# A product moved from GpSimd to VectorE in a planned schedule, with the order planned anew

## The chip, the cores and the metric

One core of a Trainium2 chip (trn2) runs the kernel. Its engines are TensorE (PE, which shows in the profile as PE for matmuls and PEld for weight loads), VectorE (DVE), ScalarE (ACT), GpSimd (POOL) and SyncE (SP, which here only issues DMAs). The metric is the device time of one execution in microseconds; a kernel is run several times and the median is given.

## The reference

A layer of 2048 tokens with 512 channels: half a feed-forward network (FFN1), a selective state-space scan, half a second feed-forward network (FFN2), each behind a layer norm and with a residual.

```python
x = x + 0.5 * ffn(layernorm(x), w1, w2, w3)
x = x + ssm(layernorm(x), W_x, W_dt, b_dt, A_log, D_param)
x = x + 0.5 * ffn(layernorm(x), w1, w2, w3)

# ffn: weights rounded to -1, 0, 1
hidden = sigmoid(x @ q(w1).T) * (x @ q(w2).T);  out = hidden @ q(w3).T

# ssm, x here is the normed x ("xln" in the kernel)
xz = x @ W_x.T                      # 128 columns dt_raw, 16 columns b, 16 columns c
dt = softplus(dt_raw @ W_dt.T + b_dt)
h[t] = exp(dt[t] * a) * h[t-1] + dt[t] * b[t] * x[t]     # a state for each of 16 n and 512 channels
y[t] = sum over n of h[t] * c[t];   out = y + x * D_param
```

The change concerns `dt * x`, called u, which is the same for all 16 states n and is multiplied by b for each.

## The kernel before

Channels lie on the partitions: 512 channels are 4 groups of 128, so a tile of one chunk is 128 x 4 x 256 = 128x1024. The tokens go in 8 chunks of 256. The body is a loop over chunks c and, in each, over 16 scan steps s, one for each state. A step is spread over engines:

- ACT computes the decays exp(dt * a) of the next step into PSUM in two halves (L767) and, between them, adds the carry from the chunk before to the first column of the scan's input (L787).
- POOL multiplies u by row b of a step two ahead (`times_b`, L1201, into the ring `dbx`; called a multiplication below) and issues the DMA that adds a product to the sum over n (`add_prod`, L1214). `add_y` (L1219) adds the sum of the odd products to that of the even ones.
- DVE runs the scan in two halves (L988, scan s.0 and s.1), multiplies the states by row c (`times_c`, L1001, product s) and saves the last column (L1006).
- SP loads the rows of b and c and stores the outputs.

Beside the scan of chunk c run, a piece at a time, FFN2 of chunk c-1, FFN1 of chunk c+1 and three layer norms: LN2 (ahead of FFN2, of chunk c-1), LN1 (ahead of the scan of chunk c+1) and LN0 (ahead of FFN1 of chunk c+3). A layer norm is a round over the engines: mean (PE), centre (DVE, L933), square (ACT, L687), fold of the squares (POOL, L308 and L310; LN0 has a fold of x as well), var (PE), std (ACT, L705), recip (DVE, L937), spread (PE), norm (DVE, L941), and for the two FFNs the split into two f16 parts, x_hi (ACT, L713) and x_lo (POOL, L1175). Mean, variance and spread of all three go through one PSUM bank, `stat`. Behind LN1 come xz (PE: dt_raw, b and c), the reads of dt_raw and of b and c (ACT, L734 and L740), z0 and z1 (PE) and the softplus into dt (ACT, `z_read`, L753, four pieces), again by way of `stat`.

An FFN is 11 up tiles of 16 matmuls (up1[h] of FFN1, up2[h] of FFN2), gated by ACT's tanh (L720) and DVE's product (hid1, hid2, L953), split by ACT (hid_hi, L728) and POOL (hid_lo, L1181; lo1, lo2 in the tables), then four down products of 22 matmuls (down1, down2) and DVE's residual in two pairs (res1, res2, L960).

Each engine runs its list in order, and waits on semaphores. Where a piece stands in the list of its engine is written in four tables, AT_PE, AT_ACT, AT_DVE and AT_POOL: an entry 10*s + p is place p (0 to 3) of scan step s, with tables of their own for the first and the last chunk. On PE, which has no part in the scan, the tables give the order alone. The program walks the places and, at each, calls the pieces that are due, in a fixed order.

The product u of chunk c+1 is computed on POOL at its place `u` by `dt_times_xln` (L1189), one instruction over 128x1024; `u` has two buffers. The first multiplication of a chunk waits for `u_done`. In chunk 0, DVE computes u in two halves ahead of the loop (`first_u_of`, L1047).

Of the kernel before, what the change touches and what calls it, by code (L numbers as in the profile page):

```python
# [17 lines left out]
ALU = mybir.AluOpType  # L18
# [4 lines left out]
NS, RANK = 16, 128  # L23
# [22 lines left out]
    down1=[123, 130, 131, 133], down1_first=[142, 143, 152, 152], down2=[153, 153, 153, 153],  # L46
    down2_last=[153, 153, 153, 153], mean0=152, mean0_first=153, mean1=140, mean1_first=153, mean2=123,
    mean2_last=153, spread0=153, spread0_first=153, spread1=143, spread1_first=153, spread2=132,
    spread2_last=153, up1=[40, 40, 53, 53, 53, 83, 83, 83, 101, 111, 112],
    up1_first=[20, 23, 23, 23, 53, 73, 73, 92, 133, 140, 142],  # L50
    up2=[140, 140, 142, 143, 150, 151, 152, 152, 152, 152, 153],
    up2_last=[153, 153, 153, 153, 153, 153, 153, 153, 153, 153, 153], var0=153, var0_first=153, var1=142,
    var1_first=153, var2=131, var2_last=153, xz=150, xz_first=153, z0=151, z0_first=153, z1=152, z1_first=153)
AT_ACT = dict(
    bc_read=102, bc_read_first=111, d_xln=152, d_xln_first=152, dt_raw=102, dt_raw_first=112,
    gate1=[1, 10, 12, 12, 21, 30, 30, 40, 40, 41, 42], gate1_first=[0, 0, 0, 10, 12, 20, 22, 22, 40, 42, 42],
    gate2=[81, 92, 110, 110, 120, 121, 130, 140, 140, 141, 142],
    gate2_last=[61, 70, 82, 90, 91, 101, 102, 111, 112, 120, 122],
    hi1=[10, 12, 21, 30, 31, 31, 40, 41, 41, 50, 50], hi1_first=[2, 11, 11, 31, 32, 40, 41, 50, 50, 50, 51],
    hi2=[112, 112, 112, 112, 130, 131, 131, 141, 141, 142, 142],  # L60
    hi2_last=[71, 81, 100, 101, 111, 112, 112, 121, 130, 130, 130], square0=130, square0_first=130, square1=81,
    square1_first=90, square2=60, square2_last=30, std0=141, std0_first=140, std1=90, std1_first=92, std2=61,
    std2_last=32, x_hi0=151, x_hi0_first=150, x_hi2=71, x_hi2_last=50, z_read=[112, 112, 120, 120],
    z_read_first=[121, 121, 121, 121])
AT_DVE = dict(
    centre0=130, centre0_first=131, centre1=81, centre1_first=82, centre2=52, centre2_last=23,
    hid1=[3, 12, 20, 22, 30, 32, 40, 41, 42, 43, 51], hid1_first=[1, 2, 10, 12, 22, 30, 40, 41, 42, 50, 51],
    hid2=[90, 110, 112, 120, 130, 131, 132, 141, 142, 143, 150],
    hid2_last=[63, 82, 92, 100, 102, 110, 112, 120, 122, 123, 123], norm0=151, norm0_first=150, norm1=93,
    norm1_first=102, norm2=71, norm2_last=50, recip0=142, recip0_first=142, recip1=92, recip1_first=101,  # L70
    recip2=70, recip2_last=42, res1=[63, 72], res1_first=[63, 80], res2=[153, 153], res2_last=[102, 133])
AT_POOL = dict(
    add_y=31, add_y_last=11, fold_sq0=141, fold_sq0_first=140, fold_sq1=82, fold_sq1_first=82, fold_sq2=51,
    fold_sq2_last=32, fold_x0=92, fold_x0_first=110, lo1=[11, 30, 40, 42, 42, 42, 42, 42, 42, 42, 50],
    lo1_first=[21, 22, 31, 32, 41, 41, 41, 41, 41, 41, 41],
    lo2=[131, 131, 141, 141, 150, 150, 150, 150, 150, 150, 150],
    lo2_last=[91, 102, 110, 120, 121, 131, 131, 131, 131, 131, 131], u=132, u_first=132, x_lo0=152,
    x_lo0_first=152, x_lo2=80, x_lo2_last=51)


# [13 lines left out]
def macaron(nc, xT, w_xT, w_dtT, b_dt, a_log, d_param, w1T, w2T, w3T, outT):  # L94
    ctx = ExitStack()
    with ctx:
# [833 lines left out]
        def _(dve):  # L930
# [162 lines left out]
            def beside_scan(c, par, now):  # L1093
# [15 lines left out]
                if not last(c):  # L1109
# [4 lines left out]
                    if now == at(AT_DVE, c, "norm1"):  # L1114
                        normalise(1, c + 1, xln)
# [219 lines left out]
```

## Time and profile before

| | |
|---|---|
| median of 3 runs | 792.58 us (787.21 to 796.45) |
| the profiled execution | 794.82 us, of which the span of the trace is 793.0 us |
| mean granted TensorE clock | 0.914 |
| busy, share of the span | PE 80%, PEld 66%, DVE 81%, ACT 72%, POOL 81% |
| u on POOL (L1189) | 7 instructions, 22.4 us in all, mean 3206 ns |
| multiplications on POOL (L1201) | 127, mean 2720 ns |
| scans on DVE (L988) with a carry | 224, mean 1277 ns |

The span runs from the first to the last instruction of the core, and the execution's time is a little longer. Busy times of POOL are rough: an instruction that stands behind a DMA issue is recorded from its own issue on, so neighbours overlap. In the trace, the scan of chunk 0 begins near 80 us, that of chunk 7 ends near 749 us; before it lie the quantisation of the weights and FFN1 of chunk 0, behind it the last LN2 and FFN2. A chunk in the middle takes about 88 us.

### The profile page before, as it was taken

Reading aid. Unit: us, or ns where it says so; the run is one execution under the profiler, and the core shown is the slowest. Engines: PE = TensorE matmul, PEld = TensorE weight load, DVE = VectorE, ACT = ScalarE, POOL = GpSimd, SP = SyncE. Lnnn points to the kernel's source line nnn. Section 1 sums busy time; section 2 is a strip of 40 time slices with the busy share of each in tenths; the row PEclk is TensorE's granted clock in tenths of the full one; section 3 lists DMA queues with packets and bytes.
Section 4 is the critical chain, followed back from the end, with each engine's and each line's share of the span. In section 5 each row is a group of like instructions: output and inputs, shape, how many; then the busy total and the mean of one; then the engine's idle time right before and its main releaser. Section 6 shows DMA issues by size and latency. Waiting matters only on the chain.

```text
span 793.0 us, 14028 instructions
## 1 busy us (share of the span) xinstructions
PE 636.6 (80%) x4872; PEld 523.8 (66%) x4872; DVE 640.2 (81%) x825; ACT 569.3 (72%) x1344; POOL 644.4 (81%) x523
## 2 busy tenths in 40 slices
PE   4798775397889987997889987988889888348898
PEld 4577653286668765876667765876667766236787
DVE  3863898899877998699878997798959997599831
ACT  5864756878786879587886879678877779377441
POOL 0181999999988999699988999799988989689812
PEclk8699997599989999899999999999989999659999
DMA  9501678887748878497748777588829766968100
GB/s 355 167 1 44 155 173 177 213 185 180 160 103 186 167 169 188 89 215 180 166 98 196 162 161 186 138 172 183 199 57 211 160 139 161 208 154 167 28 27 27
DMA packets 42438, 121.06 MB, mean 153 GB/s; under 512 B 5888, under 2 KB 14848, under 8 KB 42368
## 3 DMA queue, kind: packets, MB, share of 16 engines
q0 software_dynamic: 18864, 68.69, 46.5%
q1 hardware_dynamic: 23504, 51.49, 19.5%
q8 instruction: 38, 0.62, 0.3%
q14 instruction: 32, 0.26, 0.1%
HBM read 47.03 MB, written 4.46 MB: 65 GB/s over the span
## 4 chain that ended last, share of the span: by engine, by line
PE 30%; ACT 19%; POOL 16%; DVE 16%; issue 15%; DMA 3%; DVEq 1%; ACTq 0%; POOLq 0%
PE work L413 22%; DVE states L988 9%; POOL shared L1201 8%; PE stat L413 6%; ACT decay L767 6%; POOL shared L1214 3%; DVE shared L1001 3%; ACT shared L787 2%; ACT tanh L720 2%; DMA shared<-shared 2%; POOL square L308 2%; ACT hid_hi L728 2%; POOL hid_lo L1181 1%; ACT dt L753 1%; DVE hid L953 1%
## 5 line engine op out<-in xcount | busy, mean ns | idle before, releaser
L413 PE MATMUL work<-x_hi,q 128*128 128x256 f16 x1408 | 333.8, 284 | 39.3 <-DVE hid L953 21.3
L1201 POOL TENSOR_TENSOR shared<-u,b_row 128x1024 f32<-128x1024 f32 x127 | 345.2, 2720 | 0.5
L413 PE MATMUL work<-x_lo,q 128*128 128x256 f16 x1408 | 333.1, 284 | 0.0
L767 ACT ACTIVATE decay<-dt,a_neg 128x256 f32<-128x256 f32 (+1 forms) x512 | 220.7, 464 | 102.1 <-DVE states L988 101.4
L988 DVE TENSOR_TENSOR_SCAN states<-decay,last_state,shared 128x512 f32<-128x512 f32 x224 | 279.8, 1277 | 9.3 <-ACT shared L787 3.5
L1181 POOL TENSOR_TENSOR hid_lo<-hid,hid_hi 128x256 f16<-128x256 f32 x176 | 147.8, 1082 | 96.2 <-ACT hid_hi L728 96.0
L413 PEld LDWEIGHTS work<-x_hi,q 128*128 128x128 f16 x1408 | 143.7, 102 | 75.8 <-DVE hid L953 33.9
L413 PE MATMUL work<-hid_hi,q 128*128 128x256 f16 x693 | 159.2, 279 | 8.3 <-POOL hid_lo L1181 6.1
L1001 DVE TENSOR_TENSOR shared<-states,c_row 128x1024 f32<-128x1024 f32 x128 | 155.7, 1217 | 7.8
L413 PE MATMUL work<-hid_lo,q 128*128 128x256 f16 x693 | 158.7, 278 | 0.0
L413 PEld LDWEIGHTS work<-x_lo,q 128*128 128x128 f16 x1408 | 143.3, 102 | 22.0
L1214 POOL DMA_DIRECT2D shared<-shared x124 | 140.1, 1130 | 8.7 <-DMA shared<-shared 3.3
L953 DVE SCALAR_TENSOR_TENSOR hid<-tanh,work 128x256 f32<-128x256 f32 x176 | 71.9, 410 | 37.1 <-ACT tanh L720 36.8
L720 ACT ACTIVATE tanh<-work 128x256 f32<-128x256 f32 x176 | 63.2, 370 | 37.7 <-PE work L413 33.6
L413 PEld LDWEIGHTS work<-hid_hi,q 128*128 128x128 f16 x693 | 70.1, 101 | 20.5 <-DVE hid L953 6.0
L413 PEld LDWEIGHTS work<-hid_lo,q 128*128 128x128 f16 x693 | 69.3, 100 | 10.0
L728 ACT ACTIVATE hid_hi<-hid 128x256 f16<-128x256 f32 x176 | 66.9, 408 | 9.2 <-DVE hid L953 8.9
L787 ACT ACTIVATE shared<-last_state,shared,first_decay 128x1 f32<-128x1 f32 x224 | 73.0, 373 | 0.0
L413 PE MATMUL stat<-mean_w,square 128*128 128x1 f32 x96 | 16.6, 281 | 39.5 <-POOL square L310 35.8
L413 PE MATMUL stat<-shared,mean_w 128*128 128x256 f32 x120 | 31.1, 404 | 19.3 <-DMA shared<-shared 12.1
L413 PEld LDWEIGHTS stat<-mean_w,square 128*128 128x128 f32 x96 | 14.8, 225 | 46.5 <-POOL square L310 42.1
L988 DVE TENSOR_TENSOR_SCAN states<-decay,shared 128x512 f32<-128x512 f32 x32 | 38.1, 1220 | 4.0 <-POOL shared L1298 2.0
(118 smaller groups left out, 665.1 us busy)
## 6 DMA issues: line engine op xcount, KB each, us to landing
shared<-shared POOLq DMA_DIRECT2D x131, 512.0 KB, 5.3
b_row<-bc_dram SPq DMA_DIRECT2D x32, 512.0 KB, 5.8
c_row<-bc_dram SPq DMA_DIRECT2D x32, 512.0 KB, 6.2
x_in<-xT SPq DMA_DIRECT2D x8, 512.0 KB, 7.0
outT<-shared SPq DMA_DIRECT2D x7, 512.0 KB, 5.5
shared<-w1T SPq DMA_DIRECT2D x4, 704.0 KB, 8.5
shared<-w2T SPq DMA_DIRECT2D x4, 704.0 KB, 12.1
shared<-w3T SPq DMA_DIRECT2D x3, 768.0 KB, 13.4
```

The costliest lines, as they stand in the source:

```text
L308: engine.tensor_tensor(dst[:, 0:2, :], src[:, 0:2, :], src[:, 2:4, :], ALU.add).then_inc(summed, 1)
L413: return nc.tensor.matmul(out, lhsT, rhs, start=start, stop=stop)
L720: nc.scalar.activation(tanh[:, h % 3, :], bank_of(which, h)[:, 0, :], ACT.Tanh, scale=0.5 / X_SCALE).then_inc(tanh_done, 1)
L728: nc.scalar.activation(hid_hi[:, h, :], hid[:, hid_slot(which, h), :], ACT.Copy).then_inc(hi_done, 1)
L767: ins = nc.scalar.activation(decay[pair][:, j, j:TC], dt[:, par, k, j:TC], ACT.Exp, scale=a_neg[:, k, n:n + 1])
L787: nc.scalar.activation(column, last_state[:, n, k:k + 1], ACT.Identity, scale=first_decay[:, par, j, n:n + 1], bias=column).then_inc(carry ...
L953: nc.vector.scalar_tensor_tensor(out=hid[:, hid_slot(which, h), :], in0=tanh[:, h % 3, :], scalar=1.0, in1=bank_of(which, h)[:, 1, :], op0 ...
L988: nc.vector.tensor_tensor_scan(out=states[:, two, :].rearrange("p k t -> p (k t)"), data0=decay[pair][:, :, :].rearrange("p k t -> p (k t) ...
L1001: nc.vector.tensor_tensor(prod_of(c, n), states[:, :, :], bcast(c_row[:, group % 2, n % ROWS, :]), ALU.mult).then_inc(prod_done, 1)
L1181: nc.gpsimd.tensor_tensor(hid_lo[:, h, :], hid[:, hid_slot(which, h), :], hid_hi[:, h, :], ALU.subtract).then_inc(lo_done, 1)
L1201: nc.gpsimd.tensor_tensor(dbx[:, g % DBX_RING, :, :], u[:, par, :, :], bcast(b_row[:, group % 2, n % ROWS, :]), ALU.mult).then_inc(dbx_don ...
L1214: nc.gpsimd.dma_start(total, prod_of(c, n), accum_op=ALU.add).then_inc(added(c, n)[0], 16)
```

## The change

The product u of the chunk that comes next is taken off POOL's list and put on DVE's, at a place of its own: behind product 12 (entry 123), in chunk 0 behind scan 14.0 (entry 141). On DVE it waits for all four pieces of the softplus, and for the multiplications of the chunk before the last, which read the same buffer. All four tables are new. In a middle chunk the order of PE becomes ..., mean1, up2[0] to up2[2], var1, up2[3], spread1, xz, z0, up2[4], up2[5], z1, mean0, up2[6] to up2[8], var0, spread0, up2[9], up2[10], down2. It was ..., mean1, up2[0], up2[1], var1, up2[2], spread1, up2[3], xz, up2[4], z0, up2[5], z1, mean0, up2[6] to up2[9], var0, spread0, up2[10], down2.

```diff
 AT_PE = dict(
-    down1=[123, 130, 131, 133], down1_first=[142, 143, 152, 152], down2=[153, 153, 153, 153],
-    down2_last=[153, 153, 153, 153], mean0=152, mean0_first=153, mean1=140, mean1_first=153, mean2=123,
...
-    up2=[140, 140, 142, 143, 150, 151, 152, 152, 152, 152, 153],
...
+    down1=[133, 133, 140, 141], down1_first=[142, 150, 150, 151], down2=[153, 153, 153, 153],
+    down2_last=[153, 153, 153, 153], mean0=152, mean0_first=153, mean1=143, mean1_first=153, mean2=133,
...
+    up2=[143, 143, 143, 150, 151, 151, 152, 152, 152, 153, 153],
...
 AT_ACT = dict(
...
-    hi2_last=[71, 81, 100, 101, 111, 112, 112, 121, 130, 130, 130], square0=130, square0_first=130, square1=81,
-    square1_first=90, square2=60, square2_last=30, std0=141, std0_first=140, std1=90, std1_first=92, std2=61,
...
+    hi2_last=[82, 92, 92, 110, 110, 111, 111, 112, 120, 121, 122], square0=122, square0_first=131, square1=72,
+    square1_first=82, square2=51, square2_last=30, std0=132, std0_first=141, std1=90, std1_first=100, std2=60,
...
 AT_DVE = dict(
-    centre0=130, centre0_first=131, centre1=81, centre1_first=82, centre2=52, centre2_last=23,
...
-    hid2_last=[63, 82, 92, 100, 102, 110, 112, 120, 122, 123, 123], norm0=151, norm0_first=150, norm1=93,
-    norm1_first=102, norm2=71, norm2_last=50, recip0=142, recip0_first=142, recip1=92, recip1_first=101,
-    recip2=70, recip2_last=42, res1=[63, 72], res1_first=[63, 80], res2=[153, 153], res2_last=[102, 133])
+    centre0=130, centre0_first=133, centre1=80, centre1_first=90, centre2=51, centre2_last=22,
...
+    hid2_last=[80, 83, 92, 93, 102, 103, 112, 113, 120, 122, 130], norm0=150, norm0_first=150, norm1=93,
+    norm1_first=103, norm2=70, norm2_last=60, recip0=141, recip0_first=150, recip1=92, recip1_first=102,
+    recip2=63, recip2_last=50, res1=[63, 71], res1_first=[80, 81], res2=[153, 153], res2_last=[113, 113], u=123,
+    u_first=141)
 AT_POOL = dict(
...
-    lo2=[131, 131, 141, 141, 150, 150, 150, 150, 150, 150, 150],
-    lo2_last=[91, 102, 110, 120, 121, 131, 131, 131, 131, 131, 131], u=132, u_first=132, x_lo0=152,
-    x_lo0_first=152, x_lo2=80, x_lo2_last=51)
...
+    lo2=[131, 141, 141, 141, 141, 142, 151, 151, 151, 151, 151],
+    lo2_last=[100, 111, 111, 121, 121, 122, 122, 130, 131, 131, 131], x_lo0=152, x_lo0_first=152, x_lo2=72,
+    x_lo2_last=71)
...
+            def dt_times_xln(c, par):
+
+                dve.wait_ge(z_read, KD * (c + 1))
+                if c > 1:
+                    dve.wait_ge(dbx_done, NS * (c - 1))
+                nc.vector.tensor_tensor(u[:, par, :, :], dt[:, par, :, :], xln[:, :, :], ALU.mult).then_inc(u_done, 1)
+
...
+                    if now == at(AT_DVE, c, "u"):
+                        dt_times_xln(c + 1, 1 - par)
...
-            def dt_times_xln(c, par):
-                pool.wait_ge(z_read, KD * (c + 1))
-                nc.gpsimd.tensor_tensor(u[:, par, :, :], dt[:, par, :, :], xln[:, :, :], ALU.mult).then_inc(u_done, 1)
-
...
-                    if now == at(AT_POOL, c, "u"):
-                        dt_times_xln(c + 1, 1 - par)
```

## Rows read from the trace of the kernel before

**Rows 1.** Busy us, 228 to 317: length, PE, PEld, DVE, ACT, POOL; clock, DMA

```profile
228.00:317.00 89.00, 77.04 (x596) 63.56 (x597) 75.98 (x102) 69.55 (x169) 81.09 (x68) 0.94 0.74 162
```

**Rows 2.** DVE's waits, 228 to 317 us: waiter, releaser, us, times, longest

```profile
DVE shared L960 <- PE work L413: 3.9, 1, 3.9
DVE hid L953 <- ACT tanh L720: 3.3, 1, 3.3
DVE rstd L937 <- ACT std L705: 3.1, 2, 1.6
DVE xln L941 <- PE stat L413: 1.2, 1, 1.2
DVE centred L933 <- PE stat L413: 1.0, 1, 1.0
DVE states L988 <- ACT shared L787: 0.6, 1, 0.6
```

**Rows 3.** Timeline of PE, 286 to 318 us: start, length, operation, wait before

```profile
287.07 0.61 PE L413 MATMUL stat<-mean_w,square 128*128 128x1 f32 x4 [1.55 <-POOL square L310]
...
304.57 0.70 PE L413 MATMUL stat<-square,mean_w 128*128 128x256 f32 x2 [0.93 <-ACT dt L753]
...
313.19 0.61 PE L413 MATMUL stat<-mean_w,square 128*128 128x1 f32 x4 [0.45 <-POOL square L310]
316.62 1.22 PE L413 MATMUL stat<-ident,rstd 128*128 128x128 f32 x4 [2.83 <-DVE rstd L937]
```

**Rows 4.** Timeline of POOL, 300 to 312 us

```profile
301.24 2.94 POOL L1201 TENSOR_TENSOR shared<-u,b_row 128x1024 f32<-128x1024 f32 x1
...
305.40 3.25 POOL L1189 TENSOR_TENSOR u<-dt,xln 128x1024 f32<-128x1024 f32 x1
308.73 2.37 POOL L1201 TENSOR_TENSOR shared<-u,b_row 128x1024 f32<-128x1024 f32 x1
311.05 1.27 POOL L308 TENSOR_TENSOR square<-square 128x512 f32<-128x512 f32 x1
```

**Rows 5.** Timeline of ACT, 303 to 316 us

```profile
303.67 0.84 ACT L753 ACTIVATE dt<-stat,bdt 128x256 f32<-128x256 f32 x2
...
308.52 1.05 ACT L687 ACTIVATE square<-centred 128x1024 f32<-128x1024 f32 x1
...
314.81 1.28 ACT L705 ACT_TABLE_LOAD   x1
```

**Rows 6.** Groups of DVE by line: count, busy us, mean ns

```profile
L941 DVE TENSOR_TENSOR xln<-centred,stat 128x1024 f32<-128x1024 f32 x7 | 8.5, 1219 | 6.9 <-PE stat L413 6.9
...
L1047 DVE TENSOR_TENSOR u<-dt,xln 128x512 f32<-128x512 f32 x2 | 1.4, 686 | 2.3 <-ACT dt L852 2.3
```

**Rows 7.** Timelines of POOL and of DVE, 34 to 55 us

```profile
34.47 0.67 POOL L1181 TENSOR_TENSOR hid_lo<-hid,hid_hi 128x256 f16<-128x256 f32 x1 [33.00 <-ACT hid_hi L728]
...
45.35 9.07 POOL L1181 TENSOR_TENSOR hid_lo<-hid,hid_hi 128x256 f16<-128x256 f32 x7
...
45.89 1.81 DVE L1041 SCALAR_TENSOR_TENSOR q<-shared,thr,q 128x1536 f16<-128x1536 f32 x1
```

**Rows 8.** Busy time by engine in three stretches of 2 us

```profile
294.00:296.00 2.00, 2.00 (x10) 1.15 (x9) 1.87 (x4) 1.60 (x5) 2.00 (x3) 1.00 0.11 20
318.00:320.00 2.00, 2.00 (x12) 1.38 (x10) 0.52 (x3) 1.43 (x5) 1.29 (x2) 0.50 0.18 33
326.00:328.00 2.00, 2.00 (x21) 1.79 (x19) 1.72 (x3) 2.00 (x6) 2.00 (x2) 1.00 0.51 98
```

**Rows 9.** Timeline of PE in chunk 0: xz

```profile
127.58 3.78 PE L413 MATMUL stat<-xln,wx 128*128 128x256 f32 x8 [1.31 <-DVE xln L941]
```

**Rows 10.** DVE's waits, 78 to 142, 580 to 658 and 678 to 752 us

```profile
DVE centred L933 <- PE stat L413: 2.0, 1, 2.0
...
DVE hid L953 <- ACT tanh L720: 5.1, 2, 3.3
...
DVE centred L933 <- PE stat L413: 3.4, 1, 3.4
```

## What I expect, and why

> **What bounds the kernel now.** The granted clock and the page come first: one core, all four compute engines busy for 72 to 81% of the span (table above), no single one full. So I cut the span into chunks of tokens. Between 228 and 317 us, one steady chunk, DVE works 76 of 89 us and POOL 81 [rows 1]. POOL's share says less than it seems: its instructions overlap in the record with the DMA issues behind them. The next view is the list of DVE's waits in that chunk [rows 2]. DVE runs its list in order, the same list in every chunk; so the length of a chunk is DVE's work plus those waits, and it is there that a change must show. They are: 3.9 us for the residual's last pair (res2[1], behind PE's down products), 3.3 for the last gated tile (hid2[10]), 1.6 twice for the reciprocal of LN0's deviation (the stretch holds two chunk ends), 1.2 for LN1's spread, 1.0 for LN0's mean, 0.6 for the carry. The timeline of PE shows the chain behind most of them: the three layer norms of a chunk take turns in one PSUM bank (stat), each a round through PE, DVE, ACT, POOL and PE again. At the chunk's end PE waits 0.45 us for POOL's fold of the squares (var0) and 2.83 for the reciprocal (spread0) [rows 3]. It then still has one up tile and all of down2 to do, for which DVE waits in turn.
>
> **The product u.** POOL's seven u products go. One is issued at 305.40 and the next multiplication starts at 308.73, the fold of LN0's squares at 311.05 [rows 4]; ACT had those squares at 308.52 + 1.05 = 309.57 [rows 5]. So on POOL u holds var0 back by 1.5 us, no more. DVE adds seven u. The half-size form, the same operation on the same tensors, took 686 ns in chunk 0, and a full 128x1024 product with one operand in PSUM 1219 [rows 6]: 1.22 to 1.37 us, I take 1.22. Its place is after product 12 and ahead of centre0. It needs the last softplus, which ended at 303.67 + 0.84 = 304.51 [rows 5], and LN0's mean, for which DVE waited 1.0 us there, was waiting for the same softplus [rows 3]. So u runs in that wait and in the 0.6 us for the carry behind it. 1.6 us of waits become 1.22 of work: -0.3 a chunk (-0.4 if both go wholly, +1.2 if neither does). Queued behind u's new wait on DVE are centre0, hid2[4] and scan 13, which all waited for that softplus or for ACT behind it already. The second new wait, for an older chunk's multiplications, is long met. On POOL the next chunk's first multiplication now waits for DVE's u, and the fold is queued behind it. By the softplus u ends near 305.8, the multiplication (2.37) at 308.2, before the squares are there; POOL waits, but nobody for it.
>
> u reads two operands in SBUF, which no other DVE instruction of the scan does. The quantisation at the start does, and there the rows show a price: seven hid_lo tiles took 9.07 us where a lone one took 0.67, that is 4.4 too many, while three such DVE operations ran, the first of them 1.81 long [rows 7]. Such an operation and a reading POOL exclude each other. In the steady chunk POOL's multiplication 15, 301.24 + 2.94, has ended before u may start, and what follows is one hid_lo, a DMA issue and the multiplication that waits for u. I charge nothing here, and keep 0 to 2.4 us (one multiplication) a u for the range.
>
> The Trainium skill ("SBUF — State Buffer", Who interferes with whom) says that a DVE instruction with two SBUF inputs contends with a GpSimd instruction that reads SBUF, and that whichever issued first keeps the shared port to its end. By that rule u could stand behind a whole multiplication in each chunk, which is the second rival below; by the order in the rows it stands behind nothing. The trace agrees that there is a lock.
>
> **The new order.** Read against the old one (a table entry 10s+p is the place p of scan step s), four moves matter.
>
> LN1: centre1 goes ahead of scan 8.0, square1 ahead of ACT's step 8, var1 behind a third up2 tile. Before, PE stood 1.55 us at var1 [rows 3]; the third tile now fills that. Spread1 is then ready as DVE comes to norm1, whose wait of 1.2 us shrinks. Bounds 0 and -1.2, I take -0.9, since the fold on POOL still lies between. xz then follows spread1 without the tile that stood there, so PE waits about as long as norm1 takes, 1.2 us, twice over with the read of dt_raw. That delays up2 tiles, not the chain.
>
> LN0's deviation: std0 goes in ACT from behind the next step's decays and carry to ahead of them. Before, ACT reached it at 314.81 with the variance ready since 313.8 [rows 3, 5]; with the 1.5 us from POOL it can run near 312.5. recip0 goes one scan forward in DVE. Its wait of 1.6 us should fall to 0.3: -1.3 (bounds 0 and -1.6).
>
> The chunk's end: up2[9] goes behind spread0, where only up2[10] and down2 stood. A tile of 16 matmuls costs 1.5 us at full clock (21 in 2 us) and 2.7 at half (12 in 2 us) [rows 8]; the restart after spread0 runs at half clock (0.50, 1.2 GHz) in both orders, for the same stretch, so I charge PE 1.8. DVE has one scan and one gated tile (about 1.7 us) more between recip0 and res2[1] than before, but at the half clock both tiles come late: I take +0.5. Bounds: +1.8 if nothing covers the tile, -2.5 if the shorter stand of PE before spread0 keeps the clock up.
>
> A steady chunk so gives -0.3 - 0.9 - 1.3 + 0.5 = -2.0, and five of them (chunks 1 to 5) -10. Chunk 0 has waits of 2.0 us at centre0 [rows 10]; centre0 goes later and u in: -0.5 (-1.8 to +1.2). Chunk 6 has no LN0; its hid waits are 5.1 us [rows 10], of which 3.3 belong to the end of the chunk before, and the rest, 1.8, is where u goes; norm1 stands there as in the others: -0.6 - 0.9 = -1.5. In chunk 7 centre2 waits 3.4 us for the last sums of products [rows 10]; POOL's last multiplication of chunk 6 now stands ahead of five hid_lo tiles, so the DMA that adds the last product leaves up to 2.4 us earlier, and centre2 goes ahead of one product (1.2): -1. What moves in the last chunk's FFN2 ends where it did: hid2[10] stays behind product 12. Sum: -10 - 0.5 - 1.5 - 1 = -13 us. Start and tail are untouched. On the profiled execution, 793.0 of span in 794.82, that is 781.8; it lies 2.2 over the median of the three runs, 792.58, from which I forecast 780.
>
> **The rivals.** First, the waits only change their place. After spread0 PE has the same down2 and one tile more, and res2[1] ends the chunk; if spread0 doesn't come earlier by as much as the three waits shrink, +1.8 in place of +0.5 and -0.6 in place of -1.3 leave 0.0 a chunk, and -3 in all: 790 us. For it: res2[1] is the largest wait of the chunk, and PE's. Against it: spread0 itself hung on the reciprocal.
>
> Second, the lock. If POOL runs ahead in the new order so that a multiplication is under way at each u, DVE stands 1.2 us on the mean and POOL 1.2: about 1.5 of each pair reaches the chain, 7 x 1.5 = 10: 790 us. Against it: POOL can't start the next chunk before u.
>
> Third, slower: the clock falls ahead of xz. PE now stands before xz and again before z0, where up tiles filled it. In chunk 0, after a stand of 1.31 us, eight xz matmuls took 3.78 [rows 9], 16 would take 7.6; in the steady chunk, at clock 1.00, ten of them fit in 2 us [rows 8], so 16 take half of that or less. At the lower of the two levels (1.2 GHz) the chain through softplus, u and centre0 is then 3.8 us longer in six chunks: 792.6 - 13 + 23 = 802. It decides as soon as xz runs at 0.50. Against it: up2[0] to up2[3] run on without a stand just ahead.
>
> **How the numbers follow.** Forecast 0.50, moved waits 0.23, lock 0.10, clock 0.17. 1% is 7.9 us, about what a measurement here can tell, as the three runs lie 9 us apart. Most of the forecast's case lies under 784.7, a little of it over; the first two rivals are no change; the third is slower: 0.47, 0.35, 0.18. The range takes in the clock's case to 802. Below, if half of the bound for PE's clock came true, 5 x 2.5 more, it ends at 768.
>
> **What would show it.** In the trace after: u on DVE at 1.2 to 1.3 us, right behind the last softplus; no wait at the carry of scan 13; POOL's fold of LN0 less than 0.3 us behind its squares; DVE's waits at recip0 and norm1 under 0.5; res2[1] at 3 to 5. Wrong would be u longer than 1.5 us, xz at clock 0.50, or a sum of res2[1] and hid2[10] waits over 9 us a chunk.

## The result and the profile after

The changed kernel takes 801.34 us, the median of ten runs (798.11 to 803.56), against 794.40 us for ten runs of the kernel before on the same chip (787.21 to 796.45): a ratio of 1.0100, with a 95% interval of 1.0068 to 1.0133. It is slower by 1%, where I had forecast 780 us. Its profiled execution took 798.11 us with a span of 796.3. That is the shortest of its ten, 3.2 us under their median, so the trace below shows 3.3 us of a loss that the medians put at 6.9; where the other executions lose the rest was not recorded (their mean granted clock was 0.914 to 0.925, that of the profiled one 0.936).

The page's first part says almost nothing: POOL's share falls from 81% to 79%, DVE's rises from 81% to 82%.

```profile
PE 633.6 (80%) x4872; PEld 520.8 (65%) x4872; DVE 651.4 (82%) x832; ACT 570.6 (72%) x1344; POOL 628.9 (79%) x516
```

What says where the time went is one instruction followed through both traces. DVE's product s of chunk c (the multiplication of the states with C) occurs 128 times at the same place of the algorithm, so the differences of its start times cut both spans into comparable sections. "Chunk 0" is from its first product to the first of chunk 1, "chunks 1 to 5" from there to the first of chunk 6, "6 and 7" to the last product of all. The start lies before, the tail behind. The sections of all kernels of this study, from one profiled execution each, in us:

| kernel | start | chunk 0 | chunks 1 to 5 | chunks 6 and 7 | tail | span |
|---|---|---|---|---|---|---|
| before | 84.27 | 72.12 | 441.54 | 149.88 | 45.19 | 793.0 |
| after | 84.03 | 77.65 | 436.81 | 152.89 | 44.92 | 796.3 |
| e1 u alone, old order | 83.44 | 72.73 | 440.28 | 150.78 | 44.87 | 792.1 |
| e2 new order, u on POOL | 82.62 | 77.25 | 438.04 | 150.91 | 47.18 | 796.0 |
| e3 chunk 0 as before | 85.48 | 74.78 | 438.16 | 153.09 | 45.09 | 796.6 |
| e4 tiles ahead of xz | 83.62 | 78.32 | 433.14 | 151.77 | 47.05 | 793.9 |
| e5 first gate later | 82.60 | 75.57 | 440.99 | 152.97 | 47.07 | 799.2 |
| e6 chunk 7 as before | 85.39 | 78.12 | 438.27 | 150.36 | 45.06 | 797.2 |
| e7 both ends as before, tiles | 84.21 | 73.54 | 433.07 | 149.25 | 45.03 | 785.1 |
| e8 the same, u on POOL | 83.63 | 72.74 | 436.38 | 149.99 | 45.06 | 787.8 |
| e9 e7 with chunk 0 as changed | 83.21 | 75.25 | 435.83 | 149.27 | 45.04 | 788.6 |
| e10 e7 with half an u more | 83.67 | 75.29 | 431.23 | 149.95 | 45.26 | 785.4 |
| e11 e7 with up2[9] earlier | 84.20 | 73.62 | 430.46 | 149.39 | 44.93 | 782.6 |
| e12 up2[4] ahead of xz | 83.50 | 77.99 | 473.05 | 158.79 | 47.47 | 840.8 |
| e13 up2[3] ahead of xz | 84.70 | 77.74 | 432.26 | 151.32 | 45.08 | 791.1 |

No kernel changes the start or the tail: their spread (82.6 to 85.5; 45 or 47) is what one execution does by itself, and kernels that are alike in the middle differ there by up to 2.8 (e7, e9). So a smaller difference of one section is not read as an effect by itself, only where the rows below or the times say the same.

The middle gains 4.73 us, less than half of the 10 that I forecast. Chunk 0 loses 5.53 and chunks 6 and 7 lose 3.01.

**The middle.** DVE's waits in a steady chunk (first view, 231 to 320 us: waiter, releaser, us, times, longest) answer to [rows 2]; the second view is the busy time of that stretch, as in [rows 1].

```profile
DVE shared L961 <- PE work L414: 4.5, 2, 4.1
DVE hid L954 <- ACT tanh L721: 2.0, 3, 1.3
DVE u L1050 <- ACT dt L754: 0.9, 1, 0.9
DVE rstd L938 <- ACT std L706: 0.7, 1, 0.7
DVE centred L942 <- PE stat L414: 0.6, 1, 0.6
```
```profile
231.00:320.00 89.00, 77.00 (x603) 63.03 (x602) 78.08 (x101) 70.01 (x170) 79.05 (x68) 0.96 0.73 161
```

The wait for LN0's deviation fell from 1.6 to 0.7, that of norm1 from 1.2 to 0.6, hid2[10]'s from 3.3 to 1.7 in this chunk; res2's rose from 3.9 to 4.5; u has a wait of its own. Over chunks 1 to 5, DVE's idle time fell from 12.76 to 10.17 us a chunk (worked out from all of DVE's rows there), and its busy time rose from 75.55 to 77.19: 0.95 a chunk are left.

The timeline of TensorE (PE) shows where u's wait comes from. Here are the eight xz matmuls of all six chunks, and one chunk's rounds ahead of them (start, length, operation, wait before); [rows 3] and [rows 8] answer to them.

```profile
207.54 3.50 PE L414 MATMUL stat<-xln,wx 128*128 128x256 f32 x8 [1.78 <-DVE xln L942]
...
289.93 0.58 PE L414 MATMUL stat<-mean_w,square 128*128 128x1 f32 x4
...
293.11 0.71 PE L414 MATMUL stat<-ident,rstd 128*128 128x128 f32 x4 [0.51 <-DVE rstd L938]
295.61 3.47 PE L414 MATMUL stat<-xln,wx 128*128 128x256 f32 x8 [1.78 <-DVE xln L942]
299.01 2.08 PE L414 MATMUL stat<-xln,wbc 128*32 128x256 f32 x8
...
383.82 2.94 PE L414 MATMUL stat<-xln,wx 128*128 128x256 f32 x8 [1.78 <-DVE xln L942]
...
470.68 1.99 PE L414 MATMUL stat<-xln,wx 128*128 128x256 f32 x8 [1.78 <-DVE xln L942]
...
557.59 1.99 PE L414 MATMUL stat<-xln,wx 128*128 128x256 f32 x8 [1.78 <-DVE xln L942]
...
644.33 3.56 PE L414 MATMUL stat<-xln,wx 128*128 128x256 f32 x8 [1.78 <-DVE xln L942]
```
```profile
294.00:296.00 2.00, 0.39 (x2) 0.37 (x3) 2.00 (x4) 1.38 (x5) 2.00 (x3) 0.99 1.05 201
296.00:298.00 2.00, 2.00 (x6) 1.57 (x5) 1.93 (x2) 1.21 (x4) 1.92 (x3) 0.50 0.71 135
```

In every chunk TensorE now stands 1.78 us ahead of xz. In four of six the matmuls then run at a granted clock of 0.50 (1.2 GHz) and take 2.9 to 3.6 us; in two they take 1.99. The eight behind them (wbc) are at full speed again. DVE's rows at u show what that costs: 0.89 us of waiting in just those four chunks, none in the two others (the second row).

```profile
308.77 1.22 DVE L1050 TENSOR_TENSOR u<-dt,xln 128x1024 f32<-128x1024 f32 x1 [0.89 <-ACT dt L754]
...
482.69 1.40 DVE L1050 TENSOR_TENSOR u<-dt,xln 128x1024 f32<-128x1024 f32 x1
```

So u does not wait for the stand alone; it waits for the clock behind it. The traces of one order bear this out without moving a tile. In the changed kernel and in e3, e5 and e6 below, which leave these tiles where they are, xz ran at the lower clock for most of its length in 17 of the 24 chunks 1 to 6 (2.9 to 3.7 us) and at full speed in 7 (1.99). From product 12 to product 13 DVE takes 7.9 to 8.0 us in each of the 17 and 6.9 in each of the 7: a chunk at the lower clock pays 1.06 us there, 0.89 at u and 0.17 at the carry behind it. What decides which chunks it hits is not shown.

**The end of chunk 0**, on DVE, TensorE and POOL:

```profile
143.27 1.22 DVE L934 TENSOR_TENSOR centred<-x_in,stat 128x1024 f32<-128x1024 f32 x1 [2.53 <-PE stat L414]
...
145.54 1.21 DVE L1050 TENSOR_TENSOR u<-dt,xln 128x1024 f32<-128x1024 f32 x1
...
150.07 0.17 DVE L938 RECIPROCAL rstd<-std 128x2 f32<-128x2 f32 x1 [0.76 <-ACT std L706]
151.55 1.22 DVE L942 TENSOR_TENSOR centred<-centred,stat 128x1024 f32<-128x1024 f32 x1 [1.31 <-PE stat L414]
...
161.35 0.42 DVE L954 SCALAR_TENSOR_TENSOR hid<-tanh,work 128x256 f32<-128x256 f32 x1 [2.22 <-ACT tanh L721]
```
```profile
139.04 2.04 PE L414 MATMUL stat<-dt_raw,wdt 128*128 128x256 f32 x4 [2.67 <-ACT dt L754]
142.01 1.22 PE L414 MATMUL stat<-square,mean_w 128*128 128x256 f32 x2 [0.93 <-ACT dt L754]
148.72 1.02 PE L414 MATMUL stat<-mean_w,square 128*128 128x1 f32 x4 [5.49 <-POOL square L311]
```
```profile
145.67 2.19 POOL L309 TENSOR_TENSOR square<-square 128x512 f32<-128x512 f32 x1 [3.94 <-ACT square L688]
```

The chain mean0, squares, fold, var0, recip0, norm0 lies on DVE's path here. It starts late (mean0 at 142.01, where it was at 139.94 before), its fold takes 2.19 us beside u, where it takes 1.27 alone, and DVE waits for it three times (2.53 us at centre0, 0.76 at recip0, 1.31 at norm0). Of the 5.53 us that chunk 0 loses, 3.9 are waits of DVE and 1.6 its work, u above all. The last row of DVE is hid1[0] of chunk 1, which the new table sets ahead of the first product (place 2 for 3): the product stands behind its wait of 2.22 us.

**Chunk 7** keeps its wait at centre2 (3.4 in [rows 10], now one product earlier). The last product of chunk 6, for whose sum centre2 waits, and centre2, before and after:

```profile
671.25 1.22 DVE L1001 TENSOR_TENSOR shared<-states,c_row 128x1024 f32<-128x1024 f32 x1
...
693.84 1.22 DVE L933 TENSOR_TENSOR centred<-shared,stat 128x1024 f32<-128x1024 f32 x1 [3.37 <-PE stat L413]
```
```profile
672.47 1.23 DVE L1002 TENSOR_TENSOR shared<-states,c_row 128x1024 f32<-128x1024 f32 x1
...
694.92 1.22 DVE L934 TENSOR_TENSOR centred<-shared,stat 128x1024 f32<-128x1024 f32 x1 [3.70 <-PE stat L414]
...
719.41 0.42 DVE L954 SCALAR_TENSOR_TENSOR hid<-tanh,work 128x256 f32<-128x256 f32 x1 [1.18 <-ACT tanh L721]
```

From the one to the other it takes 22.6 us before and 22.5 after. The third row is a wait of FFN2's gates that chunk 7 did not have.

### The profile page after: what moved, and what is told of

Same layout as the page of the kernel before. It is cut to its first block, busy times and chain, and to the rows that moved or that the text cites. A ratio compares the mean times of both kernels' runs of the same rounds, so it can differ in the third digit from the quotient of the medians.

```text
span 796.3 us, 14034 instructions
## 1 busy us (share of the span) xinstructions
PE 633.6 (80%) x4872; PEld 520.8 (65%) x4872; DVE 651.4 (82%) x832; ACT 570.6 (72%) x1344; POOL 628.9 (79%) x516
## 4 chain that ended last, share of the span: by engine, by line
PE 30%; DVE 21%; POOL 17%; ACT 15%; issue 13%; DMA 3%; DVEq 1%; ACTq 0%; POOLq 0%
PE work L414 21%; DVE states L989 11%; PE stat L414 8%; POOL hid_lo L1191 7%; POOL shared L1207 5%; ACT decay L768 5%; DVE shared L1002 4%; DMA shared<-shared 2%; ACT shared L788 2%; ACT tanh L721 2%; POOL shared L1220 1%; ACT hid_hi L729 1%; POOL square L309 1%; ACT dt L754 1%; POOL shared L1253 1%
## 5 line engine op out<-in xcount | busy, mean ns | idle before, releaser
L414 PE MATMUL work<-x_hi,q 128*128 128x256 f16 x1408 | 324.3, 280 | 36.6 <-DVE hid L954 17.6
L414 PE MATMUL work<-x_lo,q 128*128 128x256 f16 x1408 | 323.6, 279 | 0.0
L1191 POOL TENSOR_TENSOR hid_lo<-hid,hid_hi 128x256 f16<-128x256 f32 x176 | 153.7, 1214 | 66.0 <-ACT hid_hi L729 66.0
L414 PEld LDWEIGHTS work<-x_hi,q 128*128 128x128 f16 x1408 | 141.2, 100 | 66.3 <-DVE hid L954 25.2
L414 PE MATMUL work<-hid_hi,q 128*128 128x256 f16 x693 | 155.4, 274 | 22.1 <-POOL hid_lo L1191 18.6
L414 PE MATMUL work<-hid_lo,q 128*128 128x256 f16 x693 | 155.4, 274 | 0.0
L414 PEld LDWEIGHTS work<-x_lo,q 128*128 128x128 f16 x1408 | 141.1, 100 | 20.2
L309 POOL TENSOR_TENSOR square<-square 128x512 f32<-128x512 f32 x21 | 33.7, 1603 | 12.8 <-ACT square L688 12.7
L1185 POOL TENSOR_TENSOR x_lo<-centred,x_hi 128x1024 f16<-128x1024 f32 x14 | 34.6, 2473 | 6.0 <-ACT x_hi L714 6.0
```

Source lines behind the costliest of these rows:

```text
L309: engine.tensor_tensor(dst[:, 0:2, :], src[:, 0:2, :], src[:, 2:4, :], ALU.add).then_inc(summed, 1)
L414: return nc.tensor.matmul(out, lhsT, rhs, start=start, stop=stop)
L1191: nc.gpsimd.tensor_tensor(hid_lo[:, h, :], hid[:, hid_slot(which, h), :], hid_hi[:, h, :], ALU.subtract).then_inc(lo_done, 1)
```

## Experiments

My theory after the result: the order costs at both ends and through the clock at xz, and the move of u is not the matter. The ratios below stand against the kernel before on the same chip, five rounds each. The runs were made on several chips, on which the kernel before took 792.5 to 795.3 us, so between runs of different chips the ratios compare better than the medians.

**e1: u alone, in the old order.**

```diff
 AT_DVE = dict(
...
+    u=130, u_first=131)
 AT_POOL = dict(
...
-    u=132, u_first=132,
```

> The old order in every list, with u alone moved from POOL to DVE, right ahead of centre0 (place 130, in chunk 0 place 131). If u is what made the change slow, because its 1.22 us on DVE is not covered, seven of them put it 4 to 9 us over the kernel before (798 to 803). If u is covered by DVE's waits for LN0's mean and the carry, as in my prediction, and the new order is what cost the time, it comes out 2 to 8 us under the kernel before, for LN0's fold on POOL is no longer behind u: 786 to 792, with POOL's fold in the middle chunks right behind ACT's squares.

795.49 us, ratio 1.0031 (1.0010 to 1.0051): between my two ranges, so neither came. All sections lie within 1.3 us of before: by itself the move gains nothing. The group of u on DVE (duration min/median/max in ns, first and last start) shows one reason:

```profile
L1048 DVE TENSOR_TENSOR u<-dt,xln x7: 1226/2020/3074, 139.5 to 654.7; 128x1024 f32<-128x1024 f32 x7
```

At this place POOL is still reading in most chunks, and u takes 2.02 us (the median) where it takes 1.21 alone. That is my second rival's lock, real in an order that was not the changed one's.

**e2: the new order with u on POOL.** The changed tables, with u and u_first taken from DVE's table and put at 132 in POOL's.

> The new order in every list, with u back on POOL at its old place (132, behind the DMA issue of product 12). If the new order lost the time, it is as slow as the changed kernel or slower by up to 8 us (800 to 809): the 5 us lost at the end of chunk 0 and the first xz matmuls at half clock stay. If u on DVE lost it, it falls back to the kernel before or under it (787 to 796).

798.31 us, 1.0063 (1.0040 to 1.0086): between the two ranges, nearer to the order's. Chunk 0 loses 5.1 us, as in the changed kernel (5.5), and xz runs at the lower clock in four of six chunks here too: those losses belong to the order. The profiled spans of e2 and of the changed kernel are equal (796.0, 796.3), the timed ratios 0.4% apart: the changed kernel's trace is of its shortest execution, 0.4% under its median, and that of e2 lies at its median (797.79).

**e3: chunk 0 in its old places** (all that end in _first), u_first at 131.

```diff
-    up1_first=[11, 23, 33, 33, 43, 112, 113, 121, 140, 140, 140],
+    up1_first=[20, 23, 23, 23, 53, 73, 73, 92, 133, 140, 142],
...
-    centre0=130, centre0_first=133,
+    centre0=130, centre0_first=131,
...
-    u_first=141)
+    u_first=131)
```

> The changed kernel with the lists of chunk 0 as they were before, and u of that chunk on DVE right ahead of centre0 (131). In the traces the changed kernel falls 5.3 us behind between product 13 of chunk 0 and product 0 of chunk 1. If the lists of chunk 0 do that, this run is 4 to 6 us faster than the changed kernel (795 to 797), and its product 0 of chunk 1 comes within 1.5 us of that of the kernel before (156.4). If u in chunk 0 does it by itself, the time stays at 799 to 803.

796.48 us, 1.0041 (1.0021 to 1.0062), as the theory said. Products 12 to 15 of chunk 0 take 16.91 us (19.62 changed, 16.27 before). Behind them, though, the step to chunk 1 still takes 6.23, against 4.10 before: hid1[0] has no place of its own for chunk 0.

**e4: TensorE's tiles around LN1 as before.**

```diff
-    down1=[133, 133, 140, 141],
+    down1=[113, 113, 120, 121],
...
-    up2=[143, 143, 143, 150, 151, 151, 152, 152, 152, 153, 153],
+    up2=[122, 122, 123, 130, 131, 132, 133, 133, 133, 153, 153],
...
-    var1=150, xz=151, z0=151, z1=152, spread1=151,
+    var1=123, xz=131, z0=132, z1=133, spread1=130,
```

> The changed kernel with PE's list around LN1 as before: up2[2] between var1 and spread1, up2[3] between spread1 and xz, up2[4] between xz and z0, up2[5] ahead of z1. In the changed kernel eight xz matmuls of a middle chunk took 3.47 us, against 1.89 before. If the stand of PE ahead of xz is what halves the clock there, the eight take 1.9 again and six chunks gain about 1.5 us each: 790 to 794. If the tile ahead of xz costs the chain as much as the clock does (one tile is 1.7 us), the time stays within 3 us of the changed kernel (798 to 804), with the clock up.

794.36 us, 1.0009 (0.9988 to 1.0029), at the edge of the theory's range. xz takes 1.9 to 2.0 us in all six chunks without a wait, u waits nowhere, and chunks 1 to 5 are 3.7 us shorter than in the changed kernel. The clock's theory holds, but three tiles moved at once (up2[2] to up2[4]), so e12 and e13 were made.

**e12 and e13: one step of that alone.** In the changed kernel's order "var1, up2[3], spread1, xz, z0, up2[4]", e12 puts up2[4] ahead of xz; e13 instead puts up2[2] behind var1 and up2[3] behind spread1.

```diff
 e12
-    up2=[143, 143, 143, 150, 151, 151, 152, 152, 152, 153, 153],
+    up2=[142, 142, 142, 143, 150, 151, 152, 152, 152, 153, 153],
 e13
-    up2=[143, 143, 143, 150, 151, 151, 152, 152, 152, 153, 153],
+    up2=[142, 142, 143, 150, 151, 151, 152, 152, 152, 153, 153],
 both
-    mean1=143, var1=150, spread1=151,
+    mean1=142, var1=143, spread1=150,
```

> The changed kernel with one tile moved: in each of chunks 1 to 6 TensorE issues up2[4] between spread1 and xz instead of behind z0; nothing else is moved against anything. Theory that what the new order loses in the middle is TensorE idle for 1.8 us ahead of xz and then on the lower clock: xz takes 1.9 us without a wait in all chunks (3.5 us in four of six before), u waits no more (0.9 us in four chunks), and the run is 2 to 4 us shorter than the changed kernel (797 to 799). Rival, that the gain of the kernel with the tiles ahead of the projections came from its other moved tiles (those ahead of LN2's sums): within 1 us of the changed kernel (800.5 to 802). Second rival, that the tile makes xz itself late, since it takes 1.9 us and the idle time is 1.8 us: xz ends where it did with the lower clock, and u waits 0.5 us or more still.

842.27 us, 1.0619 (1.0581 to 1.0656): neither theory. TensorE's timeline shows the moved tile behind spread1:

```profile
299.43 0.71 PE L414 MATMUL stat<-ident,rstd 128*128 128x128 f32 x4 [0.51 <-DVE rstd L938]
306.06 0.40 PE L414 MATMUL work<-x_hi,q 128*128 128x256 f16 x1 [5.92 <-DVE hid L954]
```

The tile needs an accumulator that a gate multiply (hid) frees, and that stands on DVE behind norm1 and a product. TensorE's list is in order, so xz and the later tiles wait behind it, and DVE then stands 5.5 to 7.1 us at a later gate, in each of six chunks. The run told nothing of the clock.

> The changed kernel with two tiles of chunks 1 to 6 each put one place later on TensorE: up2[2] behind var1 instead of ahead of it, up2[3] behind spread1 and so ahead of xz; unlike up2[4] of the run before, whose accumulator waits for a gate multiply that stands behind norm1 on VectorE, these have their accumulators free in time. Theory that the idle 1.8 us ahead of xz and the lower clock behind it are what the new order loses in the middle: xz takes 1.9 to 2.0 us in all chunks, waits under 0.2 us, u does not wait for dt, and the run is 2 to 4 us shorter than the changed kernel (797 to 799). Rival, that the gain of the kernel with the tiles ahead of the projections came from its other moved tiles: within 1 us of the changed kernel (800.5 to 802).

792.77 us, 1.0002 (0.9976 to 1.0029). These tiles have their accumulators:

```profile
288.15 0.61 PE L414 MATMUL stat<-mean_w,square 128*128 128x1 f32 x4 [1.55 <-POOL square L311]
...
291.38 1.22 PE L414 MATMUL stat<-ident,rstd 128*128 128x128 f32 x4 [0.45 <-DVE rstd L938]
...
294.63 1.89 PE L414 MATMUL stat<-xln,wx 128*128 128x256 f32 x8
```

xz takes 1.9 to 2.0 us in all chunks from 1 on, u's wait is gone, and TensorE stands 1.55 us at var1 instead, as before the change [rows 3]. The ratio falls by 1.0%, chunks 1 to 5 by 4.55 us, and they now gain 1.86 a chunk on the kernel before. So it was these two tiles; the rival that other tiles of e4 did it falls. The time fell by 8 us, more than the 2 to 4 that I expected; the two traces are 5.2 apart, and 3.2 more is what the changed kernel's trace lies under its median.

**e5: hid1[0] behind the first product again.**

```diff
-    hid1=[2, 12, 20, 21, 30, 31, 32, 40, 50, 50, 50],
+    hid1=[3, 12, 20, 21, 30, 31, 32, 40, 50, 50, 50],
```

> The changed kernel with one number put back: the first gate multiply of a chunk's first feed-forward (hid1[0]) stands behind the product of step 0 again (place 3 for 2). Theory that the end of chunk 0 lost time in two places, of which one is this multiply, which stands ahead of chunk 1's first product and waits 2.22 us there for its tanh: in chunk 1 the product of step 0 comes about 2.1 us sooner, later chunks show no wait at either place, so the run is 1 to 2 us shorter than the changed kernel (about 799.5 to 800.5). Rival, that the wait only passes on: the same wait shows up behind that product in chunk 1 and the run is within 0.5 us of the changed kernel.

797.50 us, 1.0047 (1.0030 to 1.0064), 0.5% below the changed kernel and lower than expected. The step from product 15 to the next chunk takes 4.10 us again for 6.52. But 1.5 us of waits return behind the product (0.80 at hid1[0], 0.75 at a carry), and the profiled execution, the longest of its seven, shows no gain by the chunk's end. That the place costs is shown, its size is not.

**e6: chunk 7 in its old places.**

```diff
-    centre2=51, centre2_last=22,
+    centre2=51, centre2_last=23,
...
-    hid2_last=[80, 83, 92, 93, 102, 103, 112, 113, 120, 122, 130],
+    hid2_last=[63, 82, 92, 100, 102, 110, 112, 120, 122, 123, 123],
```

> The changed kernel with the places of the last chunk (all that end in _last) as before. Theory that the new places of chunk 7 lose 1.5 us between its first and its last product (68.08 against 66.62 us): the run is 1 to 2.5 us shorter than the changed kernel (799 to 800.5), and chunk 7 takes 66.5 to 67. Rival, that chunk 7 is long for what chunk 6 hands it and not for its own order: chunk 7 stays at 68 and the run within 0.5 us of the changed kernel.

797.26 us, 1.0036 (1.0022 to 1.0051), lower than expected. From its first product to its last, chunk 7 takes 65.47 us (68.08 changed, 66.62 before). Its wait at centre2 is shorter than in both, but centre2 stands no earlier behind chunk 6's last product (22.3 us):

```profile
675.85 1.23 DVE L1001 TENSOR_TENSOR shared<-states,c_row 128x1024 f32<-128x1024 f32 x1
...
698.18 1.22 DVE L933 TENSOR_TENSOR centred<-shared,stat 128x1024 f32<-128x1024 f32 x1 [2.23 <-PE stat L413]
```

The wait is shorter because chunk 7's first product comes 0.9 us later behind that product than before, 10.8 us for 9.9. From centre2 to chunk 7's last product it takes 53.97 us, as before, where the changed kernel takes 56.47: that 2.5 is the new last table's.

**e7 and e8: both ends as before, tiles ahead of xz; then u back on POOL.**

```diff
 e7: tables ..._first and ..._last as before, up2, down1, xz as in e4, and
+    u_first=132, hid1=[3, 12, 20, 21, 30, 31, 32, 40, 50, 50, 50],
 e8: e7, and
-    u=123, u_first=132)
 AT_POOL = dict(
+    u=132, u_first=132,
```

> The changed kernel's middle chunks alone: the places of chunk 0 and of chunk 7 as before (the product dt by xln right behind centre0 in chunk 0), hid1[0] behind the product of step 0, and TensorE's first up tiles again ahead of and between the projections. Theory that the loss sits at both ends and at the projections' clock, and that the middle is worth 1.7 us for each of five chunks: 786 to 789, 5 to 8 us under the kernel before, with u at 1.2 to 1.4 us and no wait for dt in chunks 1 to 6. Rival, that what is mended at one place is waited for at the next (chunk 0's end, the tail's feed-forward): 792 to 795, no better than the kernel with the tiles alone (794.4).

786.78 us, 0.9907 (0.9890 to 0.9925): faster than both kernels, as the theory said. The medians differ by 7.9 us from before, and so do the spans.

> The run before with one thing changed: the product dt by xln goes back to GpSimd (place 132). Theory that the move itself is worth little in either order, since what VectorE gains in waits it pays in its own 1.2 us: within 2 us of the run before (786 to 791), with waits at centre0 of about 1 us and at the carry of scan 13 of 0.55 us in each chunk. Rival, that the move carries the gain of the middle chunks: 4 to 8 us slower than the run before.

792.16 us, 0.9962 (0.9943 to 0.9980). The move of u is worth 5.4 us here by the medians and 4.4 by the ratios (2.7 between the two traces): my theory falls and the rival holds. With u on POOL, centre0 and the carry wait again (0.5 and 0.56 us in chunks 2 to 4). By e1 the move alone gains nothing in the old order; it gains in this one.

**e9: e7 with chunk 0 as changed.** All places that end in _first as in the change.

> The best run so far (786.8 us: both ends as before, tiles ahead of the projections) with chunk 0 in the changed kernel's order again (all places that end in _first). Theory that the new order of chunk 0's last three steps, with the product dt by xln behind centre0 and the first scan of step 14, and recip0 and norm0 later, costs by itself: from the product of step 12 of chunk 0 to the first of chunk 1 it takes about 24 us for 22, and the run is 1.5 to 3 us slower (788.5 to 790). Rival, that only the first gate multiply cost there, which stays behind its product here: within 0.7 us of 786.8.

790.88 us, 0.9945 (0.9926 to 0.9963): over e7 by 4 us by the medians and 3 by the ratios, a little more than the theory's. Products 12 to 15 of chunk 0 take 19.64 us for 17.85. With e3, the first table's cost stands apart from hid1[0]'s.

**e10: half an u more on DVE.**

```diff
+                nc.vector.tensor_tensor(u_again[:, :, :], dt[:, par, 0:2, :], xln[:, 0:2, :], ALU.mult)
                 nc.vector.tensor_tensor(u[:, par, :, :], dt[:, par, :, :], xln[:, :, :], ALU.mult).then_inc(u_done, 1)
```

> The best run so far (786.8 us) with one more multiply ahead of each product dt by xln on VectorE: the same operands, half as long, into a buffer that nobody reads (it adds work and changes no result). It measures what VectorE's time is worth at that place: by the row of a 512-element operation it takes about 0.7 us, seven times. Theory that u sits on the path there since nothing waits at scan 13 any more: 4 to 5 us slower (791 to 792). Rival, that u and its neighbours lie in waits, as my forecast had it for the old order: within 1.5 us (786 to 788.5).

788.66 us, 0.9917 (0.9903 to 0.9930). The seven multiplies take 6.9 us (median 0.87), of which 1.9 (by the medians) or 0.8 (by the ratios) reach the time. My theory here, that u lies wholly on the path, falls, and the rival holds by the ratios. The rows of recip0 in chunk 2, of e7 and of e10, show where it went in a steady chunk: the next wait of DVE shrinks.

```profile
313.52 0.17 DVE L936 RECIPROCAL rstd<-std 128x2 f32<-128x2 f32 x1 [0.72 <-ACT std L704]
```
```profile
312.83 0.17 DVE L937 RECIPROCAL rstd<-std 128x2 f32<-128x2 f32 x1 [0.26 <-ACT std L705]
```

The shortest steady chunks last 85.6 us in both (u behind the multiply takes 1.21 us there, and 1.4 without it). Chunk 0, where u is followed by no such wait, pays instead: 75.29 us for 73.54, as the multiply takes 0.67 and u behind it 2.28 for 1.21, beside POOL's fold.

```profile
143.92 2.28 DVE L1050 TENSOR_TENSOR u<-dt,xln 128x1024 f32<-128x1024 f32 x1
```

**e11: e7 with up2[9] ahead of var0 and spread0 again.**

```diff
-    up2=[122, 122, 123, 130, 131, 132, 133, 133, 133, 153, 153],
+    up2=[122, 122, 123, 130, 131, 132, 133, 133, 133, 152, 153],
```

> The best run so far (786.8 us) with the last up tile but one of the second feed-forward (up2[9]) issued ahead of var0 and spread0 instead of behind both, as the kernel before had it. My forecast charged its new place 0.5 us a chunk. By that theory this run is about 2.5 us faster (784 to 785) and the wait of 0.5 to 1.8 us at hid2 before the last product is gone. Rival: a tile of 32 matmuls takes 3.5 us where TensorE waits 0.5 us for the folded squares, so var0 comes 3 us late, norm0 and x_hi with it, and the run is 2 to 10 us slower.

784.54 us, 0.9872 (0.9857 to 0.9887), the fastest of all. TensorE's rounds of LN0 in chunk 2, e7 first, then e11:

```profile
310.86 0.61 PE L412 MATMUL stat<-mean_w,square 128*128 128x1 f32 x4 [0.49 <-POOL square L309]
313.74 0.71 PE L412 MATMUL stat<-ident,rstd 128*128 128x128 f32 x4 [2.27 <-DVE rstd L936]
```
```profile
311.88 0.50 PE L412 MATMUL stat<-mean_w,square 128*128 128x1 f32 x4
312.94 0.71 PE L412 MATMUL stat<-ident,rstd 128*128 128x128 f32 x4 [0.55 <-DVE rstd L936]
```

The tile fills the stand at spread0 (2.27 to 0.55), recip0 waits 0.2 us longer, and the wait at hid2 ahead of the last product is 0.5 in every chunk, where it went up to 1.8. A gain of 2.6 us in five chunks (2.8 by the ratios of e7 and e11), as large as my term said.

The cause, though, is the clock. In the 4 us behind spread0 the granted clock of e7 is 1.00 in chunks 2 and 3 and 0.57 to 0.78 in chunks 1, 4 and 5; that last gate waits 0.52 us in the two and 1.5 to 1.8 in the three (e7, chunks 2 and 4):

```profile
318.81 0.42 DVE L952 SCALAR_TENSOR_TENSOR hid<-tanh,work 128x256 f32<-128x256 f32 x1 [0.52 <-ACT tanh L719]
...
491.56 0.42 DVE L952 SCALAR_TENSOR_TENSOR hid<-tanh,work 128x256 f32<-128x256 f32 x1 [1.83 <-ACT tanh L719]
```

In e11, with the stand at 0.55 us, the clock there is 1.00 in all five. Its chunks all last 85.8 to 86.0 us, counted from product 10 to product 10; in e7 the two at 1.00 last 85.6 and the other three 86.6 to 87.2.

## Why the forecast was wrong

Term by term, in us of the profiled execution (by the medians the loss is 6.9 us and not 3.3); the last column is what the term gives once its cause is taken away:

| term | forecast | measured | in which run it is mended |
|---|---|---|---|
| chunks 1 to 5 | -10 | -4.7 | -9.3 (e13), -11.1 (e11) |
| chunk 0 | -0.5 | +5.5 | +1.4 (e7) |
| chunks 6 and 7 | -2.5 | +3.0 | +0.5 (e6), -0.6 (e7) |
| start, tail | 0 | -0.5 | |
| sum | -13 | +3.3 | -7.9 (e7), -10.4 (e11) |

**The step that failed in the middle** is the sentence "That delays up2 tiles, not the chain." I saw that xz would lose the tile ahead of it and costed TensorE's stand, by itself rightly at nothing, but not the clock behind it; I had that as the third rival, and "xz at clock 0.50" as a sign of being wrong. Its mechanism came true, in four of six chunks, at another price: not 3.8 us in every chunk but 1.06 in each that it hit (4.55 in five chunks by e13, the tiles' other effects included), since only eight matmuls were slow, not sixteen. That the time came out near the rival's 802 is chance: 23 us at xz were forecast there, and in the trace some 5 at xz and 8.5 in the chunks at the ends came.

**The step that failed at the ends** is the size of three small terms, and in one of them, chunk 7's, the mechanism. For chunk 0 I wrote "centre0 goes later and u in: -0.5 (-1.8 to +1.2)" and read two of its places; recip0_first went from 142 to 150, behind a product, and hid1[0] ahead of one. It cost 5.5. Products 12 to 15 take 3.35 longer (19.62 against 16.27), of which the first table gives back 2.7 (e3; 1.8 by e9 against e7); the 0.6 left is u's. The step to chunk 1 takes 2.4 longer (6.52 against 4.10) with hid1[0] ahead of the product, of which e5's trace pays 1.5 behind it. For chunk 7 I wrote -1, since "the DMA that adds the last product leaves up to 2.4 us earlier". It did leave earlier, 2.1 us behind the start of chunk 6's last product for 3.9 before, but its landing, for which POOL's `add_y` waits, came only 0.4 earlier (`add_y` is issued 9.9 us behind that start for 10.3), and the mean behind `add_y`'s own DMA 0.1 earlier (18.7 for 18.8). So centre2 gained 0.1 and not 1. The new last table, which I had costed at nothing, adds 2.5: centre2 ahead of a product that it need not hold, and a new wait of 1.2 at hid2_last. In chunk 6 u didn't go into the waits: DVE idles 10.02 us there for 10.34 and works 1.9 more.

**What held.** u takes 1.2 us on DVE (median 1226 ns) and the carry of scan 13 waits at most 0.18 for 0.55 in chunks 1 to 5. The fold follows the squares at once (313.86, with them ready at 313.78). Norm1's wait fell by 0.6 (forecast 0.9), recip0's by 0.9 (forecast 1.3), and res2[1] took 4.1 (forecast 3 to 5). And a steady chunk of this order, without the two tiles' mistake, gains 1.9 of my 2.0.

**What was luck.** That 1.9 is not made of my terms. From the kernel before to e13, as means of DVE's waits and work in chunks 1 to 5, u costs 0.3 where I had -0.3 (waits of 1.3 went, 1.6 of work came, most of it u), norm1 gives 0.75 for 0.9 and recip0 0.86 for 1.3. The chunk's end, which I had charged with 0.5, gives 0.6: hid2's waits fell by 1.3 and res2's rose by 0.75. I had taken the restart behind spread0 at half clock "in both orders, for the same stretch"; it was not the same. So the charge of 0.5 for up2[9] had the right size (e11: 0.52 a chunk) by another cause, the clock in three chunks of five.

**The lock**, my second rival, costs the changed kernel little (six of seven u's up to 1.4 us, one 1.66), but it is what u alone runs into (e1). In e13 the multiplication 15 of chunk 6 is under way as u is issued:

```profile
652.55 2.62 DVE L1050 TENSOR_TENSOR u<-dt,xln 128x1024 f32<-128x1024 f32 x1
```
```profile
650.82 2.64 POOL L1207 TENSOR_TENSOR shared<-u,b_row 128x1024 f32<-128x1024 f32 x1
653.14 0.94 POOL L1191 TENSOR_TENSOR hid_lo<-hid,hid_hi 128x256 f16<-128x256 f32 x1
```

u takes 1.4 us longer than alone, as if it had begun when these two of POOL had ended (654.1). This agrees with what the Trainium skill says ("SBUF — State Buffer", Who interferes with whom): a DVE instruction with two SBUF inputs and a GpSimd one that reads SBUF exclude each other, and the first to issue keeps the port. That POOL's second instruction also went ahead of the waiting u is read from u's length alone.

Three things stay open: what the changed kernel's other executions lose beyond its trace (3.2 us at the median), what decides in which chunks the clock falls, and how much of e5's 0.5% is hid1[0]'s.

## What to carry to other kernels

A change of order is costed at its ends as carefully as in its middle: the first chunk and the last two lost nearly twice what the five steady ones gained. A tile that stands ahead of short matmuls for whose result others wait can be there to hold the clock up, and whether another one can take its place depends on which accumulator is free at that moment. An instruction that moves to a fuller engine pays only where that engine would wait anyway: the same move was worth nothing in the old order and 4 to 5 us in the mended one. A DMA that is issued earlier is worth what it lands earlier, and a forecast that comes out in its sum is to be compared term by term all the same.

## What the hardware showed that I had not expected

The clock does not fall each time: behind stands of 0.51 and 1.78 us with 0.7 us of work between them, xz ran at 1.2 GHz in four chunks and at 2.4 GHz in two of the same execution. A fold on POOL that was issued 0.13 us behind a 1.21 us multiply of DVE took 2.19 us, and 1.27 alone; in e13 it was DVE's multiply, issued while POOL's was under way, that took longer. And of 6.9 us of work added to an engine that is busy for 84% of the span, at most 1.9 were seen in the time. A DMA that left 1.8 us earlier landed 0.4 us earlier, and `add_y`'s own took 8.6 us to land where the next product's was issued 2.7 us behind it (the changed kernel) and 4.6 where that came only after its landing (e2, e8).
